# Causal mask of the diagonal score blocks added by VectorE instead of by TensorE, with another plan of the stretches and a norm's scale on GpSimd

## The chip, the cores and the metric

One core of one Trainium2 chip runs the whole program in one launch. The metric is the device time of one execution in microseconds (us), and lower is better. TensorE (PE), VectorE (DVE), ScalarE (ACT), GpSimd (POOL) and SyncE (SP, which here only issues transfers) each run their own instruction stream in order and wait for each other by semaphores.

## What is computed

```python
xn = _layernorm(x)                              # x: (4, 1024, 1024) float32
# attention: 32 query heads, 8 key/value heads, head size 32, causal
q, k, v = rope(xn @ wq.T), rope(xn @ wk.T), xn @ wv.T      # split into heads
scores = einsum('bhtd,bhsd->bhts', q, k) / sqrt(32)
scores = scores + triu(full((T, T), -inf), k=1)
s = (einsum('bhts,bhsd->bhtd', softmax(scores), v)) @ wo.T
# gate: a small recurrence on the last position of each batch row
x_norm = layer_norm(xn, in_gamma, in_beta)
thought = x_norm[:, -1, :] @ agg_w + agg_b      # (4, 1024)
for _ in range(4):
    t = layer_norm(thought, pn_gamma, pn_beta)
    t = gelu(t @ d1_w + d1_b)                   # 1024 -> 4096
    thought = thought + (t @ d2_w + d2_b)       # 4096 -> 1024
broadcast = (thought @ bc_w + bc_b)[:, None, :]
g = silu(layer_norm(xn + sigmoid(xn @ gate_w + gate_b) * broadcast, out_gamma, out_beta))
return x + s * g
```

## The kernel before

There are three phases: `project_phase` (norm, transposes and the projections to q, k, v, left in DRAM), `attention_phase` (attention, with the recurrence on `thought` woven into it), and `output_phase` (gate, output projection, norm, result). The change lies in the second.

The attention phase has 32 **turns**, one for each pair of a batch row and a key/value head, with its four query heads side by side. Turns come in pairs of one loop body (`par` 0 and 1); four pairs make one step of the recurrence, and four steps the phase. In a turn TensorE writes 36 **score blocks** into PSUM: block `u` is keys of tile `j` against queries of tile `i` (`i >= j`), 128 keys by 4 heads x 128 queries, 128x512 float32. They alternate between two banks `stp0` and `stp1` (`scores`, L1012). ScalarE takes the exponential of each block into `pr` (L800), and TensorE may write block `u + 2` only when the exponential of block `u` has released the bank. Eight of the 36 blocks are **diagonal** (`i == j`: blocks 0, 4, 7, 9, 26, 30, 33 and 35). For these TensorE adds the mask with a second product into the same bank, the identity times `mask_k` (L1015).

Everything else of a turn hangs in the gaps between score blocks. `PLAN_TEXT` says behind which block, its **slot**, each piece is issued, on TensorE and, in the same order of slots, on VectorE and ScalarE:

- `mx k`: the row maximum piece `k` (22 a turn, from 128x128 to 128x1024) is a product into `mxp0` or `mxp1` by TensorE (L999 to L1005) and a masked maximum by VectorE (L884). Piece `k` may be written when VectorE has released piece `k - 2`. Pieces 0 to 19 belong to the next turn, 20 and 21 to this one. `mt`: the maxima are transposed by TensorE, copied by ScalarE (L775) and moved by a DMA of SP (`qs<-mt`, L616) to where the next score blocks read them as an extra row.
- `pv half j`: probabilities times values (L1024). `cy`: ScalarE copies their sum out.
- `ss half`: TensorE sums the probabilities over the keys (L1033), and `rc half`: VectorE inverts them (L869 to L874). GpSimd adds the probability pieces up before that (L727, L741, L751: seven additions of half 1 and three of half 0) and multiplies the output by the inverse (L720).
- `fa`, `fb`, `fc`, `fs`, `ft`: one chunk of the recurrence's matrix products (L1055), its partial sums (L891) and its transpose; VectorE then adds the bias (`hpre`, L965) or adds to `th` (L967). `ge`: ScalarE's Gelu, with a table load on either side, in turns of `par` 0.
- `ls`, `l0`, `lc`, `l1`, `lv`, `lt`: the norm at a step's end, in the last turn of each step. `lt` is its last part: with `rs` (the reciprocal deviation, GpSimd, L715) VectorE scales, multiplies by gamma and adds beta (L861 to L863), and TensorE's first `fa` of the next turn needs the result `t_in`.

The program on VectorE is one stream: an instruction that waits holds all behind it.

Of the kernel before, what the change touches and what calls it, by code (L numbers as in the profile page):

```python
# [10 lines left out]
ALU = mybir.AluOpType  # L11
# [56 lines left out]
PLAN_TEXT = """  # L68
0: mx 20
1: pv 1 6, pv 1 7, cy 1  # L70
2: mx 21
3: fa 0, fa 1, fc
5: mx 0
6: mt 1, pv 0 0
7: mx 1
8: mx 2
9: fb 0, fb 1, fs
11: mx 3, pv 0 1, pv 0 2
12: mx 4
13: ft, pv 0 3, cy 0  # L80
14: mx 5, ls
15: mx 6
16: ss 1, rc 1
17: mx 7
18: pv 1 0
19: mx 8, l0, lc, ge
20: mx 9
21: ss 0, rc 0
22: mx 10
23: mx 11, pv 1 1, pv 1 2  # L90
24: mx 12, l1, lv
25: mx 13
26: mt 0
27: mx 14
28: mx 15, pv 1 3
29: mx 16
30: mx 17
31: pv 1 4
32: mx 18, lt
34: mx 19, pv 1 5  # L100
"""
# [27 lines left out]
def build_kernel(nc, x, wqT, wkT, wvT, woT, in_g, in_b, agg_w, agg_b, pn_g, pn_b, d1_w, d1_b, d2_w, d2_b,  # L129
                 bc_b, gate_w, gate_b, out_g, out_b, rope_c, rope_s, pick, out):  # L130
    def dram(name, shape, dt):
        return nc.dram_tensor(name, shape, dt, kind="Internal").ap()

    xt_d = dram("xt_scratch", (B, 2, P, KT, T), F32)

    q_d = dram("q_scratch", (B * PAIRS, 2, 2, P, T), F32)
    k_d = dram("k_scratch", (B, 2, 2, P, T), F32)
    v_d = dram("v_scratch", (GROUPS, P, NT, HD), F32)
    y_d = dram("y_scratch", (1 + GROUPS, P, T), F32)

    with ExitStack() as outer:
        def osb(name, shape, dt):
            return outer.enter_context(nc.sbuf_tensor(name, shape, dt))

        ident = osb("ident", [P, P], F32)
        ident16 = osb("ident16", [P, P], BF16)
# [4 lines left out]
        project_phase(nc, x, wqT, wkT, wvT, rope_c, rope_s, xt_d, q_d, k_d, v_d,  # L151
                      ident, ident16, mask_q, mask_k, mhalf)
        bcast = osb("bcast", [P, B, D], F32)
        attention_phase(nc, x, in_g, in_b, agg_w, agg_b, pn_g, pn_b, d1_w, d1_b, d2_w, d2_b, bc_b, pick,
                        q_d, k_d, v_d, y_d, ident, ident16, mask_q, mask_k, mhalf, bcast)
        output_phase(nc, x, woT, gate_w, gate_b, out_g, out_b, xt_d, y_d, mhalf, bcast, out)


def project_phase(nc, x, wqT, wkT, wvT, rope_c, rope_s, xt_d, q_d, k_d, v_d,
                  ident, ident16, mask_q, mask_k, mhalf):  # L160

# [5 lines left out]
    with ExitStack() as ctx:  # L167
# [95 lines left out]
        def _(pool):  # L263
# [10 lines left out]
                                    pattern=[[1, P]], channel_multiplier=-1).then_inc(const_ready, 1)  # L274
            pool.wait_ge(const_ready, 7)
            nc.gpsimd.tensor_copy(ident16[:], ident[:]).then_inc(const_ready, 1)

# [134 lines left out]
        def _(pe):  # L412
# [18 lines left out]
            ws = (w1, w2)  # L431
            pe.wait_ge(const_ready, 8)
            for k in range(KT):
# [40 lines left out]
def attention_phase(nc, x, in_g, in_b, agg_w, agg_b, pn_g, pn_b, d1_w, d1_b, d2_w, d2_b, bc_b, pick,  # L474
                    q_d, k_d, v_d, y_d, ident, ident16, mask_q, mask_k, mhalf, bcast):

# [6 lines left out]
    with ExitStack() as ctx:  # L483
# [211 lines left out]
        def _(pool):  # L695
# [34 lines left out]
            def turn(s, c, par, use):  # L730
# [12 lines left out]
                for j in (1, 2, 3, 4):  # L743
# [10 lines left out]
                    if j == 2:  # L754
                        normalise(0, n)
                    if j == 3 and "l1" in use:
                        ln_pool(s + 1, tb + use["l1"])

# [7 lines left out]
        def _(act):  # L766
# [18 lines left out]
            def turn(s, c, par, use):  # L785
# [3 lines left out]
                for u, (half, j, i) in enumerate(ST):  # L789
                    act.wait_ge(st_done, NST * n + u + 2)  # L790
                    if u == 0:
# [36 lines left out]
        def _(dve):  # L828
# [30 lines left out]
            def layernorm_scale(k, base):  # L859
                dve.wait_ge(ln_rs, k + 1)  # L860
                link(nc.vector.tensor_tensor(cen[:], cen[:], rows(rs[:]), ALU.mult), base)  # L861
                link(nc.vector.tensor_tensor(cen[:], cen[:], bc(fvec[:, 1, :], B), ALU.mult), base)
                nc.vector.tensor_tensor(t_in[:, :, 0:B], cen[:], bc(fvec[:, 2, :], B), ALU.add).then_inc(t_done, 1)  # L863

# [58 lines left out]
            for k in range(MX_LATE + 1):  # L923
# [6 lines left out]
                elif step == 1:  # L930
                    add_burst(3)
                elif step == 2:
                    chunk_out(4, 0)
                    dve.wait_ge(c_in, 16 * 12)
                    link(nc.vector.tensor_tensor(th[:], fr[:], bc(fvec[:, 0, :], B), ALU.add), 0)
                    layernorm_sum()
                elif step == 3:
                    layernorm_centre(5, 0)
                elif step == 4:
                    layernorm_var(6)  # L940
                    layernorm_scale(0, 0)
                if k < MX_LATE:
                    row_max(k, k, 0)
            BASE = links["n"]
            def turn(s, c, par, use):
# [6 lines left out]
                for slot in PLAN:  # L952
                    for e in slot:
                        if e[0] == "mx":
                            ahead = e[1] < MX_LATE
                            row_max(e[1], (n + ahead) * NMX + e[1], 1 - par if ahead else par)
                        elif e[0] == "rc":
                            reciprocals(e[1], n, tb + use[("ss", e[1])])
# [29 lines left out]
        def _(pe):  # L988
# [467 lines left out]
```

## Time and profile before

| | |
|---|---|
| median of 3 runs | 2692.56 us (2688.55 to 2693.68) |
| profiled execution, its time | 2689.99 us |
| its span, first to last instruction | 2687.9 us |
| busy in the span | PE 2545.3, DVE 1761.2, POOL 1370.4, ACT 994.7 us |
| attention phase, about | 606 to 1924 us, with a tail to 1950 us |

A row of the time-ordered view gives the start, the duration, the engine, the line and operation, what is written and read, and in brackets how long the engine had been idle before it and which engine and line ended that. "Busy" of PE holds modelled ends of pipelined products, so that the distance from one start to the next tells more of a product's cost than its duration does.

### The profile page before, as it was taken

To read this page: it belongs to the slowest core of one execution; us is meant where nothing else is said; L and a number is where in the kernel's file an instruction comes from. 1 tells how busy PE (TensorE), PEld (TensorE's weight loads), DVE (VectorE), ACT (ScalarE), POOL (GpSimd) and SP (SyncE) were. 2 spreads that over 40 slices of the span, in tenths; PEclk is the share of its full clock that TensorE was granted. 3 is DMA by queue.
4 is the path that set the end of the run, shared out by engine and by line. 5 is a ranking of instruction groups with operands and counts; after the bars stand their busy time and mean duration, and the time that the engine had idled before them with its cause. 6 is when DMAs were issued, how large, how long until landed. Compare 5 with 4: busy or idle time off the path is not lost. (4 is left out here: it accounts for less than half of the span.)

```text
span 2687.9 us, 45256 instructions
## 1 busy us (share of the span) xinstructions
PE 2545.3 (95%) x14205; PEld 1684.8 (63%) x14205; DVE 1761.2 (66%) x3577; ACT 994.7 (37%) x1650; POOL 1370.4 (51%) x627
## 2 busy tenths in 40 slices
PE   5999999987999989999999999999859999999998
PEld 4888888873444444444444444444348888888886
DVE  6444444537676677677677677677657777777777
ACT  2111111112566656565566555666431111111111
POOL 1111111123888888988888897898711111111111
PEclk9999999997999999999999999999879999999999
DMA  6444444438456546555456645555375666656556
GB/s 245 170 180 179 167 162 163 161 124 259 147 169 198 170 143 200 164 163 187 146 168 194 185 146 181 169 160 185 115 234 119 125 123 117 117 117 117 117 117 124
DMA packets 229848, 432.05 MB, mean 161 GB/s; under 512 B 17252, under 2 KB 100340, under 8 KB 229736
## 3 DMA queue, kind: packets, MB, share of 16 engines
q1 hardware_dynamic: 156344, 378.75, 42.9%
q0 software_dynamic: 73392, 51.91, 12.9%
q8 instruction: 58, 0.95, 0.1%
q14 instruction: 54, 0.44, 0.1%
HBM read 316.56 MB, written 113.51 MB: 160 GB/s over the span
## 5 line engine op out<-in xcount | busy, mean ns | idle before, releaser
L884 DVE CUSTOM_DVE_ANT_0 bcast<-mxp,mask_q 128x128 f32<-128x128 f32 (+7 forms) x1054 | 751.7, 751 | 347.2 <-PE mxp L1005 179.8
L800 ACT ACTIVATE pr<-stp 128x512 f32<-128x512 f32 x1152 | 665.0, 598 | 544.7 <-PE stp L1012 345.2
L1012 PE MATMUL stp<-qs,ks 97*128 97x512 f32 x1152 | 517.3, 460 | 27.8 <-ACT pr L800 19.5
L427 PE MATMUL eo<-xt,w 128*128 128x512 f32 x1920 | 448.5, 392 | 3.6 <-DVE xt L370 3.6
L751 POOL TENSOR_TENSOR acc<-acc,pr 128x2048 f32<-128x2048 f32 x96 | 440.1, 4585 | 7.5 <-POOL acc L751 4.4
L1012 PEld LDWEIGHTS stp<-qs,ks 97*128 97x128 f32 x1152 | 214.9, 189 | 356.3 <-ACT pr L800 253.8
L427 PEld LDWEIGHTS eo<-xt,w 128*128 128x128 f32 x1920 | 358.6, 189 | 77.3 <-issue 4.0
L1374 PE MATMUL gp<-g,xa 128*128 128x512 f32 x1536 | 355.8, 391 | 17.3 <-DMA xa<-xt_scratch 17.3
L1374 PE MATMUL op<-o,ya 128*128 128x512 f32 x1536 | 355.9, 391 | 10.2 <-DVE ya L1317 10.2
L1374 PEld LDWEIGHTS gp<-g,xa 128*128 128x128 f32 x1536 | 290.0, 189 | 78.4 <-DMA xa<-xt_scratch 18.1
L1374 PEld LDWEIGHTS op<-o,ya 128*128 128x128 f32 x1536 | 290.1, 189 | 70.9 <-DVE ya L1317 10.6
L1024 PE MATMUL yp<-pr,vs 128*32 128x512 f32 (+3 forms) x3088 | 315.6, 505 | 0.9 <-ACT pr L800 0.7
L727 POOL TENSOR_TENSOR acc<-acc,pr 128x1536 f32<-128x1536 f32 (+2 forms) x99 | 235.5, 2379 | 16.8 <-PE yp L1103 9.0
L292 POOL TENSOR_TENSOR r<-rt,r 128x1024 fp32r<-128x1024 f32 x40 | 96.0, 2399 | 282.0 <-ACT r L323 282.0
L1268 POOL DMA_DIRECT2D yr<-y_scratch x33 | 30.5, 924 | 363.8 <-issue 313.6
L751 POOL TENSOR_TENSOR acc<-pr 128x2048 f32<-128x2048 f32 x32 | 146.5, 4579 | 114.7 <-ACT pr L800 114.7
L396 DVE TENSOR_TENSOR rt<-eo,cs 128x512 f32<-128x512 f32 x160 | 99.0, 680 | 146.6 <-PE eo L427 146.6
L1002 PE MATMUL mxp<-ks,qs 96*128 96x512 f32 x394 | 178.2, 452 | 5.8 <-DVE mx L884 5.5
L323 ACT ACTIVATE r<-rt 128x1024 fp32r<-128x1024 f32 x40 | 42.4, 1060 | 355.4 <-DVE rt L400 350.8
L1301 ACT ACTIVATE c<-a 128x1024 f32<-128x1024 f32 x32 | 33.9, 1061 | 344.4 <-DVE a L1353 344.4
L1005 PE MATMUL mxp<-ks,qs 96*128 96x256 f32 (+2 forms) x528 | 127.9, 345 | 20.7 <-DMA qs<-q_scratch 16.2
L1024 PEld LDWEIGHTS yp<-pr,vs 128*32 128x32 f32 x3088 | 71.9, 110 | 114.6 <-issue 62.8
(143 smaller groups left out, 2991.0 us busy)
## 6 DMA issues: line engine op xcount, KB each, us to landing
wch<-in_d_w SPq DMA_DIRECT2D x132, 1024.0 KB, 10.0
qs<-q_scratch SPq DMA_DIRECT2D x201, 256.0 KB, 7.3
xa<-xt_scratch POOLq DMA_DIRECT2D x66, 512.0 KB, 6.3
xt_scratch<-xt SPq DMA_DIRECT2D x16, 2048.0 KB, 14.0
q_scratch<-r SPq DMA_DIRECT2D x64, 512.0 KB, 3.2
yr<-y_scratch POOLq DMA_DIRECT2D x33, 512.0 KB, 5.9
xs<-in_x SPq DMA_DIRECT2D x33, 512.0 KB, 5.5
y_scratch<-ys SPq DMA_DIRECT2D x65, 256.0 KB, 2.1
```

The lines of the kernel that those rows point to most:

```text
L292: nc.gpsimd.tensor_tensor(r2[:], rt[:, 0:2, :], f32(r1[:]), ALU.subtract).then_inc(r2_done, 1)
L396: last = nc.vector.tensor_tensor(rt[:, o, :], bank[:, e, :], cs[:, s, tok], ALU.mult)
L427: last = nc.tensor.matmul(out, lhs[a](k), rhs[c](k), start=(k == 0 and (a, c) == (0, 0)), stop=(k == KT - 1 and (a, c) == (1, 0)))
L727: nc.gpsimd.tensor_tensor(acc[:, :, c0:HALF], acc[:, :, c0:HALF], pr[1][:, :, at:at + HALF - c0], ALU.add).then_inc(add_done, 1)
L751: nc.gpsimd.tensor_tensor(acc[:], other, pr[1][:, :, at:at + HALF], ALU.add).then_inc(add_done, 1)
L800: nc.scalar.activation(pr[half][:, :, at:at + P], stp[u % 2][:].rearrange("p (h t) -> p h t", h=REP), ACT.Exp, scale=SCALE).then_inc(act_d ...
L884: last = nc.vector.tensor_tensor_reduce(out=bcast[:, k % 2, hh * step:hh * step + w], in0=mxp[k % 2][:, hh * step + c0:hh * step + c0 + w] ...
L1002: nc.tensor.matmul(bank[:, 0:512], lhs, ks[par][0:QR, 0:512], start=True, stop=True)
L1005: last = nc.tensor.matmul(bank[:, hh * step:hh * step + w], lhs, ks[par][0:QR, 0:w], start=True, stop=True)
L1012: last = nc.tensor.matmul(bank, ks[par][:, j * P:(j + 1) * P], qs[par][:, i // 4, :, (i % 4) * P:(i % 4 + 1) * P], start=True, stop=i != j)
L1024: last = nc.tensor.matmul(yp[h * HD:(h + 1) * HD, c0:HALF], vs[par][:, j, :], pr[half][:, h, at:at + HALF - c0], start=(j == 0), stop=(j = ...
L1374: last = nc.tensor.matmul(bank[:, cols], lhs[pa][:, k, :], ws[pw][:, k, cols], start=(k == 0 and (pa, pw) == (0, 0)), stop=(k == KT - 1 an ...
```

## The change

The mask product is gone from `scores`. Each diagonal block gets a plan entry `dm u` at its own slot: VectorE waits for the block, adds `mask_k` to it in PSUM in place (128x512, both banks as the block falls), and ScalarE's exponential waits for this instead of for TensorE. The bfloat16 identity `ident16` and its copy at the start go. The three instructions of `lt` go from VectorE to GpSimd, right behind L715, and the whole group now stands one addition earlier there (behind the second large addition instead of the third). The plan is written anew: most pieces stand at other slots.

```diff
@@ plan (two lines of each) @@
-9: fb 0, fb 1, fs
-13: ft, pv 0 3, cy 0
+9: dm 9, mx 3, mx 4
+10: ft, pv 0 0
...
@@ GpSimd @@
             def ln_pool(k, tu):
                 pool.wait_ge(tr_free, tu + 2)
                 nc.gpsimd.tensor_tensor(rs[:], ve[:], mhalf[:], ALU.pow).then_inc(ln_rs, 1)
+                pool.wait_ge(ln_rs, 3 * k + 1)
+                nc.gpsimd.tensor_tensor(cen[:], cen[:], rs[:].unsqueeze(1).to_broadcast([P, KT, B]),
+                                        ALU.mult).then_inc(ln_rs, 1)
+                pool.wait_ge(ln_rs, 3 * k + 2)
+                nc.gpsimd.tensor_tensor(cen[:], cen[:], fvec[:, 1, :].unsqueeze(2).to_broadcast([P, KT, B]),
+                                        ALU.mult).then_inc(ln_rs, 1)
+                pool.wait_ge(ln_rs, 3 * k + 3)
+                nc.gpsimd.tensor_tensor(t_in[:, :, 0:B], cen[:], fvec[:, 2, :].unsqueeze(2).to_broadcast([P, KT, B]),
+                                        ALU.add).then_inc(t_done, 1)
...
                     if j == 2:
                         normalise(0, n)
-                    if j == 3 and "l1" in use:
-                        ln_pool(s + 1, tb + use["l1"])
+                        if "l1" in use:
+                            ln_pool(s + 1, tb + use["l1"])
...
@@ ScalarE @@
-                    act.wait_ge(st_done, NST * n + u + 2)
+                    if i == j:
+                        act.wait_ge(dm_done, len(DIAG) * n + DIAG.index(u) + 1)
+                    else:
+                        act.wait_ge(st_done, NST * n + u + 2)
...
@@ VectorE @@
+                        elif e[0] == "dm":
+                            bank = stp[e[1] % 2][:].rearrange("p (h t) -> p h t", h=REP)
+                            dve.wait_ge(st_done, NST * n + e[1] + 2)
+                            nc.vector.tensor_tensor(bank, bank, mask_k[:].unsqueeze(1).to_broadcast([P, REP, P]),
+                                                    ALU.add).then_inc(dm_done, 1)
...
@@ TensorE @@
-                last = nc.tensor.matmul(bank, ks[par][:, j * P:(j + 1) * P], qs[par][:, i // 4, :, (i % 4) * P:(i % 4 + 1) * P],
-                                        start=True, stop=i != j)
-                if i == j:
-                    last = nc.tensor.matmul(bank, ident16[:], mask_k[:].unsqueeze(1).to_broadcast([P, REP, P]),
-                                            start=False, stop=True)
-                last.then_inc(st_done, 1)
+                nc.tensor.matmul(bank, ks[par][:, j * P:(j + 1) * P], qs[par][:, i // 4, :, (i % 4) * P:(i % 4 + 1) * P],
+                                 start=True, stop=True).then_inc(st_done, 1)
```

TensorE's stream of a `par` 0 turn of the kernel before, blocks 8 and 9 and what stands behind them. L1012 is a score block, L1015 the mask product, L1055 the chunk's products (`fb`).

```order
L1005 MATMUL mxp<-ks,qs 128x384 x2
L1010 REGISTER_ALU
L1012 MATMUL stp<-qs,ks 128x512
L1015 MATMUL stp<-mask_k,ident 128x512
L1038 REGISTER_ALU
L1055 MATMUL trp<-wch,t_in 32x512 x8
L1010 REGISTER_ALU
L1012 MATMUL stp<-qs,ks 128x512
```

The same engine and the same block 9 in the changed kernel, where a score block is L1019 and a row maximum product L1012. L1067 is the transpose `ft` and L1027 is `pv 0 0`.

```order
L1019 MATMUL stp<-qs,ks 128x512
L1000 REGISTER_ALU
L1012 MATMUL mxp<-ks,qs 128x384 x2
L1000 REGISTER_ALU
L1012 MATMUL mxp<-ks,qs 128x512 x2
L1017 REGISTER_ALU
L1019 MATMUL stp<-qs,ks 128x512
L1041 REGISTER_ALU
L1067 MATMUL trp<-ident,fsb 128x128 x4
L1127 ISA
L1027 MATMUL yp<-pr,vs 32x512 x4
```

Behind block 9 the chunk's products are gone (half of them stands at slot 6 and half at slot 7), the mask product is gone, and two row maxima and the transpose stand there.

VectorE's stream of the changed kernel around the same place: L964 is the new mask addition of block 9, L889 a row maximum, L903 reads the transpose and L974 is `hpre` (L965 before). Before, `hpre` stood at slot 13, behind three row maxima more than `fs`.

```order
L896 TENSOR_TENSOR fsb<-trp,fsb 128x512
L963 REGISTER_ALU
L964 TENSOR_TENSOR stp<-stp,mask_k 128x512
L884 REGISTER_ALU
L889 ISA bcast,mx<-mxp,mask_q 128x384
L889 ISA mx 128x1
...
L903 TENSOR_REDUCE fr<-trp 128x16 x2
L905 REGISTER_ALU
L973 ISA
L974 TENSOR_TENSOR hpre<-fr,b1c 128x32
```

The addition stands right in front of `mx 3` and `mx 4`, and `hpre` right behind these two.

GpSimd's stream of the changed kernel at a step's end, behind the second large addition (L759) and the product with the inverse (L728):

```order
L759 TENSOR_TENSOR acc<-acc,pr 128x2048
L726 REGISTER_ALU
L728 TENSOR_TENSOR ys<-ys,rinv 128x512
L713 REGISTER_ALU
L714 TENSOR_TENSOR f_rs<-f_ve,mhalf 128x4
L715 ISA
L716 TENSOR_TENSOR cen<-cen,f_rs 128x32
L718 REGISTER_ALU
L719 TENSOR_TENSOR cen<-cen,fvec 128x32
L721 REGISTER_ALU
L722 TENSOR_TENSOR t_in<-cen,fvec 128x8x4
```

Before, only the first of the four (`f_rs`) stood on this engine, one large addition later, and the other three on VectorE between two row maxima of slots 31 and 34.

## Rows read from the trace of the kernel before

**Rows 1.** The page: busy time, share of the span, instructions.

```profile
PE 2545.3 (95%) x14205; PEld 1684.8 (63%) x14205; DVE 1761.2 (66%) x3577; ACT 994.7 (37%) x1650; POOL 1370.4 (51%) x627
```

**Rows 2.** Busy time by stretch: span, PE, PEld, DVE, ACT, POOL, granted clock, DMA share.

```profile
768.00:846.00 78.00, 76.29 (x502) 37.55 (x501) 54.86 (x150) 46.88 (x85) 70.23 (x25) 1.00 0.57 176
...
924.00:1012.00 88.00, 81.01 (x507) 38.90 (x505) 63.49 (x157) 47.80 (x87) 72.71 (x26) 0.96 0.52 158
```

**Rows 3.** SP in order of time: one load of vs per turn, as a turn marker.

```profile
769.21 0.35 SPq L585 DMA_DIRECT2D vs<-v_scratch  x1
...
847.01 0.35 SPq L585 DMA_DIRECT2D vs<-v_scratch  x1
...
924.64 0.46 SPq L585 DMA_DIRECT2D vs<-v_scratch  x1
...
1012.38 0.35 SPq L585 DMA_DIRECT2D vs<-v_scratch  x1
```

**Rows 4.** TensorE in order of time: the waits of a pair of turns.

```profile
826.15 0.44 PE L999 MATMUL mxp<-ks,qs 96*128 96x384 f32 x1 [0.43 <-DVE mx L884]
...
829.86 0.50 PE L1012 MATMUL stp<-qs,ks 97*128 97x512 f32 x1 [1.12 <-ACT pr L800]
```

**Rows 5.** ScalarE in order of time: the first of two loads before that wait.

```profile
826.37 1.28 ACT L818 ACT_TABLE_LOAD   x1
```

**Rows 6.** Groups by form, 606 to 1924 us: count, busy us, mean ns, idle.

```profile
L751 POOL TENSOR_TENSOR acc<-acc,pr 128x2048 f32<-128x2048 f32 x96 | 440.1, 4585 | 7.5 <-POOL acc L751 4.4 <-ACT pr L800 1.1
...
L1015 PE MATMUL stp<-mask_k,ident 128*128 128x512 bf16 x256 | 101.2, 395 | 0.0
...
L884 DVE CUSTOM_DVE_ANT_0 bcast<-mxp,mask_q 128x512 f32<-128x512 f32 x132 | 85.8, 687 | 39.2 <-PE mxp L1005 38.6
...
L891 DVE TENSOR_TENSOR fsb<-trp,fsb 128x512 f32<-128x512 f32 x33 | 22.8, 692 | 12.9 <-PE trp L1055 12.9
```

**Rows 7.** TensorE and ScalarE in order of time: blocks 26 and 28, a `pv`.

```profile
1037.21 0.41 PE L1012 MATMUL stp<-qs,ks 97*128 97x512 f32 x1
1037.47 0.39 PE L1015 MATMUL stp<-mask_k,ident 128*128 128x512 bf16 x1
...
1038.54 0.51 PE L1012 MATMUL stp<-qs,ks 97*128 97x512 f32 x1
...
1039.48 1.06 PE L1024 MATMUL yp<-pr,vs 128*32 128x512 f32 x8
...
1037.89 0.60 ACT L800 ACTIVATE pr<-stp 128x512 f32<-128x512 f32 x1 [0.23 <-PE stp L1015]
```

**Rows 8.** GpSimd in order of time: late additions, and its wait in each turn.

```profile
1009.08 7.32 POOL L727 TENSOR_TENSOR acc<-acc,pr 128x1536 f32<-128x1536 f32 x3
...
1029.06 4.59 POOL L751 TENSOR_TENSOR acc<-pr 128x2048 f32<-128x2048 f32 x1 [4.84 <-ACT pr L800]
```

**Rows 9.** VectorE in order of time: `th` and `hpre` in two normal turns.

```profile
782.78 0.19 DVE L967 TENSOR_TENSOR th<-th,fr 128x32 f32<-128x32 f32 x1
...
820.94 0.72 DVE L965 TENSOR_TENSOR hpre<-fr,b1c 128x32 f32<-128x32 f32 x1
```

**Rows 10.** A step's end in order of time: GpSimd, VectorE, TensorE.

```profile
958.57 4.53 POOL L751 TENSOR_TENSOR acc<-acc,pr 128x2048 f32<-128x2048 f32 x1
...
944.71 1.39 DVE L852 TENSOR_TENSOR sq<-cen 128x32 f32<-128x32 f32 x1
...
959.65 3.50 DVE L861 TENSOR_TENSOR cen<-cen,f_rs 128x32 f32<-128x32 f32 x1
...
963.58 0.58 PE L1012 MATMUL stp<-qs,ks 97*128 97x512 f32 x1 [2.65 <-issue]
```

**Rows 11.** The tail in order of time: TensorE, and GpSimd's last product.

```profile
1922.88 0.39 PE L1015 MATMUL stp<-mask_k,ident 128*128 128x512 bf16 x1
...
1931.59 3.64 PE L1055 MATMUL trp<-wch,h_in 128*32 128x512 f32 x16 [6.77 <-DVE h_in L981]
...
1943.59 1.27 POOL L720 TENSOR_TENSOR ys<-ys,rinv 128x512 f32<-128x512 f32 x1 [10.67 <-DVE rinv L874]
```

More of the change, by code:

```diff
@@ L51 @@
 HALF_ST = len(score_units(0))
+DIAG = [u for u, (_, j, i) in enumerate(ST) if i == j]
 LAST_UNIT = {(half, j): u for u, (half, j, _) in enumerate(ST)}
@@ L68 @@
 PLAN_TEXT = """
[L69 to L76, printed above, removed]
-9: fb 0, fb 1, fs
-11: mx 3, pv 0 1, pv 0 2
-12: mx 4
-13: ft, pv 0 3, cy 0
[L81 to L86, printed above, removed]
-20: mx 9
[L88 to L100, printed above, removed]
+0: dm 0, mx 20, fa 0, fa 1
+1: mx 21, fc
+2: pv 1 6
+4: pv 1 7, mt 1, dm 4, mx 0
+5: cy 1, mx 1
+6: fb 0
+7: dm 7, mx 2, fb 1
+8: fs
+9: dm 9, mx 3, mx 4
+10: ft, pv 0 0
+12: mx 5, ls
+13: mx 6
+14: ss 1
+16: pv 0 1
+17: rc 1
+18: mx 7, mx 8, l0, lc
+19: pv 0 2
+20: mx 9
+21: mx 10
+22: pv 0 3
+23: cy 0
+24: mx 11, mx 12
+26: ss 0, dm 26, rc 0, pv 1 0
+27: mx 13, l1, lv
+28: ge, mx 14
+29: pv 1 1, pv 1 2
+30: dm 30, mx 15, mx 16
+31: pv 1 3
+32: mx 17, mt 0
+33: dm 33, mx 18
+34: pv 1 4, pv 1 5
+35: dm 35, mx 19
 """
@@ L145, in build_kernel @@
         ident = osb("ident", [P, P], F32)
-        ident16 = osb("ident16", [P, P], BF16)
         mask_q = osb("mask_q", [P, T], BF16)
@@ L151, in build_kernel @@
         project_phase(nc, x, wqT, wkT, wvT, rope_c, rope_s, xt_d, q_d, k_d, v_d,
-                      ident, ident16, mask_q, mask_k, mhalf)
+                      ident, mask_q, mask_k, mhalf)
         bcast = osb("bcast", [P, B, D], F32)
         attention_phase(nc, x, in_g, in_b, agg_w, agg_b, pn_g, pn_b, d1_w, d1_b, d2_w, d2_b, bc_b, pick,
-                        q_d, k_d, v_d, y_d, ident, ident16, mask_q, mask_k, mhalf, bcast)
+                        q_d, k_d, v_d, y_d, ident, mask_q, mask_k, mhalf, bcast)
         output_phase(nc, x, woT, gate_w, gate_b, out_g, out_b, xt_d, y_d, mhalf, bcast, out)
 def project_phase(nc, x, wqT, wkT, wvT, rope_c, rope_s, xt_d, q_d, k_d, v_d,
-                  ident, ident16, mask_q, mask_k, mhalf):
+                  ident, mask_q, mask_k, mhalf):
     NB = 2 * B
@@ L274, in _ @@
                                     pattern=[[1, P]], channel_multiplier=-1).then_inc(const_ready, 1)
-            pool.wait_ge(const_ready, 7)
-            nc.gpsimd.tensor_copy(ident16[:], ident[:]).then_inc(const_ready, 1)
             def rstd_of(n):
@@ L431, in _ @@
             ws = (w1, w2)
-            pe.wait_ge(const_ready, 8)
+            pe.wait_ge(const_ready, 7)
             for k in range(KT):
@@ L474, in attention_phase @@
 def attention_phase(nc, x, in_g, in_b, agg_w, agg_b, pn_g, pn_b, d1_w, d1_b, d2_w, d2_b, bc_b, pick,
-                    q_d, k_d, v_d, y_d, ident, ident16, mask_q, mask_k, mhalf, bcast):
+                    q_d, k_d, v_d, y_d, ident, mask_q, mask_k, mhalf, bcast):
     QR = 3 * HD
@@ L548, in attention_phase @@
         st_done, act_done, add_done, add0_done = sem("a_st"), sem("a_act"), sem("a_add"), sem("a_add0")
+        dm_done = sem("a_dm")
         mx_done, mx_free = sem("a_mx"), sem("a_mx_free")
@@ L857, in layernorm_var @@
                 nc.vector.tensor_scalar(ve[:], trp[:, 0:B], EPS_F, None, ALU.add).then_inc(tr_free, 1)
[L859 to L863, printed above, removed]
             def reciprocals(half, k, tu):
@@ L940, in _ @@
                     layernorm_var(6)
-                    layernorm_scale(0, 0)
                 if k < MX_LATE:
@@ L974, in turn @@
                             layernorm_var(tb + use["l1"])
-                        elif e[0] == "lt" and "l1" in use:
-                            layernorm_scale(s + 1, base)
                 if par == 1:
@@ L1183 @@
 LINKS_TURN = 1
-LINKS_STEP = 4
+LINKS_STEP = 2
 def output_phase(nc, x, woT, gate_w, gate_b, out_g, out_b, xt_d, y_d, mhalf, bcast, out):
```

## Prediction, made before the changed kernel ran

> **What bounds the kernel now.** I read the page first, then the busy time by stretch, then one engine after the other in order of time. The page [rows 1] has PE busy for 95% of the span, DVE for 66%, POOL for 51%. The stretches [rows 2] put that right: POOL hardly works outside the attention phase. In an undisturbed stretch of 78 us, which is a pair of turns, PE is busy 76.3 us, POOL 70.2, DVE 54.9, ACT 46.9. The change touches the bound, TensorE, but GpSimd stands close behind. The turn markers [rows 3] give 77.80 us for a normal pair (769.21 to 847.01), 38.9 a turn, and 87.74 for the pair that holds a step's end (924.64 to 1012.38), 9.9 more, at a mean clock of 0.96 instead of 1.00 [rows 2]. There are three such ends inside the phase and a fourth in its tail.
>
> What PE waits for in a normal pair is little [rows 4]: 0.43 us for a row maximum and 1.12 us for ScalarE. The second follows Gelu [rows 5]: a table load of 1.28 us on either side of it stands in front of an exponential whose bank TensorE wants. The rest, 77.80 - 1.55 = 76.25 or 38.1 us a turn, is TensorE's own work.
>
> **The mask products.** Eight a turn, 256 in all [rows 6]. The mean of 395 ns is a duration with a pipeline in it. A block of the same 512 columns lets the next product start after 0.26 us (1037.21 to 1037.47 [rows 7]), so I take 0.24 for a mask product, between 0.21 (a tenth of the distance off for the change of weights) and 0.26. That is 1.9 us a turn. TensorE's own work falls to 38.1 - 1.9 = 36.2 us a turn.
>
> **The mask additions.** No row adds from PSUM into PSUM. The nearest reads PSUM and SBUF at the same size, 692 ns (L891 [rows 6]), and the row maximum of 512 columns with the same bfloat16 mask takes 687. I take 0.69. Below, nothing in the rows suggests less than 0.6; above, the bound is twice the row, 1.4. DVE's work goes from 54.86 / 2 = 27.4 to 27.4 + 8 x 0.69 = 32.9 us a turn. It still has 3 us to spare, but it is one stream, and TensorE and ScalarE now wait for it eight times more.
>
> The chain of a diagonal block grows. Before [rows 7]: block at 1037.21, mask at 1037.47, exponential 1037.89 to 1038.49, the block after next at 1038.54, so 1.33 us. After: about 0.45 until the block has ended, 0.69 for the addition, 0.60 for the exponential and some 0.10 of signals, 1.85 us, if VectorE is free. TensorE has to have 1.85 us of work from one block to the one after the next, or more where a row maximum (0.7 to 1.2) is ahead of the addition. I went through the new plan slot by slot. The prices: 0.24 for a block, 0.44 for a row maximum of middle size [rows 4], 1.06 for a `pv` or `ss` of full width [rows 7]. Up to the block after next, block 26 has 2 x 0.24 + 1.06 (`ss 0`) + 1.06 (`pv 1 0`) + 0.44 = 3.0 us; block 30 has 2 x 0.24 + 2 x 0.44 + 1.06 = 2.4; block 33 has 2 x 0.24 + 0.44 + 1.06 and the somewhat narrower `pv 1 5`, 2.7; block 0 has `fa`, which is longer than a `pv`. Block 9 has 2 x 0.24 + 2 x 0.44 + 1.06 and the transpose, 2.7; there VectorE comes late, since `mx 2`, `fs` and the addition stand in a row, and it just suffices. Blocks 4 and 7 have about 2 us, block 35 has the row maximum and `fa`. So a few tenths a turn remain exposed, not eight times 0.5. `mt` and its DMA through SP's queue come earlier for half 1 and later for half 0 (slot 32); some 3 us of TensorE work stand between that copy and the next turn, enough for the move. The loads of k, q and v are issued by the same conditions as before.
>
> **Gelu.** `ge` now stands behind block 28, where slots 29 to 31 have three `pv` and two `mx` besides three blocks, 3 x 1.06 + 2 x 0.44 + 3 x 0.24 = 4.8 us, against 2 x 1.28 us of loads, Gelu and one exponential. The 1.12 us per pair should go, and is in the figure above already, because I took the recorded waits off.
>
> **GpSimd's floor.** POOL has 70.23 / 2 = 35.1 us a turn, and some tenths between its instructions (7.5 us in front of 96 additions alone [rows 6]), so 35.4 to 36.0. What it waits now is up to 4.84 us a turn, for the exponential that opens half 1 [rows 8]. At TensorE's 36.2 that wait is gone nearly, and GpSimd works without a pause: the turn can't fall below about 36.
>
> **What that triggers.** VectorE's `hpre` took 0.72 us where `th`, of the same size, took 0.19 [rows 9]; `cen` took 3.50 and ended when GpSimd's addition of 958.57 + 4.53 = 963.10 did [rows 10]. Both read two tensors in SBUF. With GpSimd busy all the time, `hpre` and the addition to `th`, now at slot 10, fall on one of its additions of 1.3 to 3.5 us each turn, and `mx 5` and all behind it wait. The slack of slots 11 to 17 takes most of that; I count 0 to 1.5 us a turn, and 0.5 together with the exposed tenths. The sum for a normal turn is 36.2 + 0.5 = **36.7 us**, 2.2 less than 38.9, and 32 x 2.2 = 70 us.
>
> The Trainium skill (SBUF — State Buffer, "Who interferes with whom") says that a VectorE instruction with two SBUF inputs waits for a whole GpSimd instruction that reads SBUF, and one with at most one SBUF input never does. By that rule the trace's 3.50 is a lock, and the new mask addition (one input in PSUM) stays at its price; were it locked as `cen` is, eight waits of 1 to 4 us a turn would turn the sum into a loss of several hundred us.
>
> **The norm at a step's end.** Before, `cen` and the next of the three took about 3.5 us each behind GpSimd's additions, PE waited 2.65 us [rows 10] and more behind it, and the mean clock of the pair was 0.96 [rows 2]. On GpSimd they wait for no one. Their cost there is not in the trace; the additions go at 4585 ns for 2048 elements [rows 6], 2.2 ns each, so 32 elements are below 0.3 us and each with its hand-over below 1: one to three us a step, on an engine that has a little room in hand. But `sq` (1.39 us [rows 10]) reads two SBUF inputs and now stands at slot 18, just as GpSimd begins its 4.6 us addition: up to 3 us of VectorE held, and `ls` at slot 12 can be held too. Of the 9.9 us I take back 5, three times: 15 us, with 0 and 9.9 each as bounds.
>
> **The tail.** PE waited 6.77 us for `h_in`, queued on VectorE behind the same three instructions [rows 11]. That goes, but the last step then waits for GpSimd's late additions (7.32 us [rows 8]) to reach the last sums: GpSimd has less lead than before. From the last block (1922.88) to the last product by the inverse (1943.59) 20.7 us; I take 3 off.
>
> **Sum.** 2690 - 70 - 15 - 3 = 2602 us against the profiled execution of 2689.99. The median of the runs shown lies 2.6 us above that, so **2604 us**, 3.3% faster. The identity's copy at the start is worth nothing measurable.
>
> **Rivals.**
> - *At the floor* (15%): no lock hits and no tenths are exposed, 36.2 a turn, and the ends give all 9.9. 2690 - 86 - 30 - 4 = 2570, plus 2.6: 2573. For it: the slack of slots 11 to 17. Against: VectorE at 33 of 36 us in one stream.
> - *VectorE's queue* (24%): the lock on `hpre` and `th` lasts 2 to 3 us in most turns, or the additions come late behind row maxima, so that 37.7 or more is a turn, and the ends give nothing: 2690 - 38 - 3 + 2.6 = 2652. For it: rows 9 and 10. Against: a turn made longer lets GpSimd get ahead, so that the next `hpre` meets a shorter addition.
> - *No change* (3%): the exposed waits eat exactly the 2.8 us a turn.
> - *Slower* (8%): the exposed chain at the diagonal blocks. If each of the eight costs the 0.5 us by which it is longer and half a row maximum (0.5) in front of the addition, a turn gains 8 and loses 2.7: 38.9 + 5.3, and 2690 + 32 x 5.3 = 2860. It decides from 2.7 / 8 = 0.34 us per block on. Against: the work that stands behind each diagonal block in the plan.
> - My forecast, 36.3 to 37.4 a turn, 2590 to 2626: 50%.
>
> **Numbers.** A measurement of this kernel can tell about 0.2%, 5 us. The range reaches to the floor and to VectorE's queue: 2570 to 2652, with a tenth or so outside on each side. Faster 0.89, same 0.03, slower 0.08.
>
> **What the profile after would show.** No L1015 row; PE near 36.2 us a turn of work. If I am right: turn markers at 36.3 to 37.4 us, without the 1.12 us wait behind Gelu; POOL busy above 34.5 of 36.7 us and its wait for the exponential under 1 us; mask additions at 0.69 us; no TensorE wait over 1 us in a normal turn; `hpre` often above 0.72; a step's end less than 6 us longer than a normal pair; `sq` at 2 us or more. Wrong would be: mask additions of 1 us and more, or TensorE idle in front of the block after each diagonal one (the exposed chain), or a wait for `mx` at slots 18 to 24 of a us or more in each turn (the lock).

## The result and the profile after

The changed kernel takes 2674.16 us (median of 7 runs, 2667.57 to 2679.28) against 2692.56 before (7 runs, 2688.55 to 2697.55): a ratio of 0.9929 (0.9914 to 0.9945), 0.7% faster. The forecast was 2604, and its range ended at 2652.

The page, with the lines that answer to [rows 1] and [rows 6], and the queue that brings instructions (packets, MB, share):

```profile
PE 2516.4 (94%) x13949; PEld 1667.3 (62%) x13949; DVE 1918.4 (72%) x3818; ACT 997.6 (37%) x1650; POOL 1373.6 (51%) x641
...
q14 instruction: 95, 0.78, 0.1%
...
L811 ACT ACTIVATE pr<-stp 128x512 f32<-128x512 f32 x1152 | 659.5, 597 | 513.9 <-DVE stp L964 326.9
...
L964 DVE TENSOR_TENSOR stp<-stp,mask_k 128x512 f32<-128x512 f32 x256 | 178.3, 696 | 80.3 <-PE stp L1019 44.0
```

The 256 mask products are gone and PE is busy for 28.9 us less in all, at a price of 0.696 us of VectorE for each addition, as forecast. The instruction queue moved 95 packets; its row in the page of before has 54:

```profile
q14 instruction: 54, 0.44, 0.1%
```

Next, SyncE's turn markers, which answer to [rows 3]:

```profile
764.73 0.35 SPq L584 DMA_DIRECT2D vs<-v_scratch  x1
...
806.72 0.36 SPq L584 DMA_DIRECT2D vs<-v_scratch  x1
845.25 0.35 SPq L584 DMA_DIRECT2D vs<-v_scratch  x1
882.51 0.35 SPq L584 DMA_DIRECT2D vs<-v_scratch  x1
920.08 0.35 SPq L584 DMA_DIRECT2D vs<-v_scratch  x1
966.85 0.36 SPq L584 DMA_DIRECT2D vs<-v_scratch  x1
1003.86 0.35 SPq L584 DMA_DIRECT2D vs<-v_scratch  x1
```

Turns are no longer alike. From 845.25 on they take 37.26 and 37.57 us, 74.83 the pair against 77.80 before. The pair ahead of them takes 41.99 and 38.53, 80.52. The pair with the step's end takes 83.78, 8.95 more than a good one. Busy time by stretch, with the columns of [rows 2]:

```profile
845.25:920.08 74.83, 73.23 (x486) 36.02 (x486) 66.84 (x165) 47.22 (x85) 70.70 (x25) 1.00 0.60 184
764.73:845.25 80.52, 75.93 (x486) 36.99 (x485) 66.16 (x165) 47.13 (x85) 70.01 (x25) 0.96 0.55 171
797.00:817.00 20.00, 16.82 (x94) 7.88 (x93) 12.68 (x42) 8.68 (x17) 15.46 (x7) 0.83 0.66 196
920.08:1003.86 83.78, 78.11 (x490) 37.46 (x490) 68.30 (x171) 47.22 (x85) 70.98 (x29) 0.94 0.55 165
```

The long pair does the same 486 products in 2.7 us more of busy time at clock 0.96, and is idle for 3 us more. In the 20 us around 807 the mean granted clock is 0.83, which is about 7 us at the lower level (1.2 GHz) and the rest at 2.4. What happened there, in order of time on three engines:

```profile
799.61 0.40 PE L1010 MATMUL mxp<-ks,qs 96*128 96x512 f32 x1
803.19 0.58 PE L1019 MATMUL stp<-qs,ks 97*128 97x512 f32 x1 [3.18 <-ACT pr L811]
...
801.64 0.70 DVE L964 TENSOR_TENSOR stp<-stp,mask_k 128x512 f32<-128x512 f32 x1 [3.68 <-issue]
...
802.54 1.09 ACT L811 ACTIVATE pr<-stp 128x512 f32<-128x512 f32 x2 [5.11 <-DVE stp L964]
```

Read it backwards. TensorE stood 3.18 us for an exponential; ScalarE stood 5.11 us for a mask addition; VectorE stood 3.68 us for "issue", that is, for nothing that the trace holds. The addition is the first instruction of a pair of turns (`dm 0`), the place where VectorE's loop jumps back. The phase has eight such jumps inside its steps. At six of them VectorE stands 3.5 to 3.9 us in front of the addition and TensorE then waits 2.8 to 3.4 us; at the first jump of the first and of the third step it is 2.1 and 2.0 us, and 1.4 and 1.3 us of TensorE.

Other rows in order of time, for the steps of the prediction: a normal pair's waits of TensorE (as [rows 4]), `th` beside GpSimd's addition (as [rows 9]), a step's end (as [rows 10]) and the tail (as [rows 11]):

```profile
754.74 0.50 PE L1019 MATMUL stp<-qs,ks 97*128 97x512 f32 x1 [0.72 <-ACT pr L811]
780.16 0.44 PE L1006 MATMUL mxp<-ks,qs 96*128 96x384 f32 x1 [0.68 <-DVE mx L889]
...
772.89 2.38 POOL L749 TENSOR_TENSOR acc<-acc,pr 128x1024 f32<-128x1024 f32 x1 [0.16 <-POOL acc L749]
...
772.98 2.34 DVE L976 TENSOR_TENSOR th<-th,fr 128x32 f32<-128x32 f32 x1
...
936.18 1.73 DVE L863 TENSOR_TENSOR sq<-cen 128x32 f32<-128x32 f32 x1
...
948.00 0.24 POOL L716 TENSOR_TENSOR cen<-cen,f_rs 128x32 f32<-128x32 f32 x1
948.31 0.24 POOL L719 TENSOR_TENSOR cen<-cen,fvec 128x32 f32<-128x32 f32 x1
948.63 0.24 POOL L722 TENSOR_TENSOR t_in<-cen,fvec 128x32 f32<-128x32 f32 x1
...
958.70 0.79 PE L1019 MATMUL stp<-qs,ks 97*128 97x512 f32 x1 [3.57 <-issue]
...
1912.76 3.61 PE L1058 MATMUL trp<-wch,h_in 128*32 128x512 f32 x16 [0.97 <-DVE h_in L988]
...
1923.33 1.27 POOL L728 TENSOR_TENSOR ys<-ys,rinv 128x512 f32<-128x512 f32 x1 [3.16 <-DVE rinv L879]
```

`th` needs 0.19 us alone and here 2.34, ending with GpSimd's addition. The three instructions of the norm take 0.24 us each on GpSimd. TensorE's wait for `h_in` shrank from 6.77 to 0.97 us. At the step's end TensorE still waits for "issue", 3.57 us where it was 2.65.

### The profile page after: what moved, and what is told of

Its sections match the earlier page's. It is cut to its first block and busy times, and to the rows that moved or that the text cites. A ratio compares the mean times of both kernels' runs of the same rounds, so it can differ in the third digit from the quotient of the medians.

```text
span 2668.1 us, 45287 instructions
## 1 busy us (share of the span) xinstructions
PE 2516.4 (94%) x13949; PEld 1667.3 (62%) x13949; DVE 1918.4 (72%) x3818; ACT 997.6 (37%) x1650; POOL 1373.6 (51%) x641
## 5 line engine op out<-in xcount | busy, mean ns | idle before, releaser
L889 DVE CUSTOM_DVE_ANT_0 bcast<-mxp,mask_q 128x128 f32<-128x128 f32 (+7 forms) x1054 | 749.8, 750 | 110.6 <-PE mxp L1010 67.3
L1019 PE MATMUL stp<-qs,ks 97*128 97x512 f32 x1152 | 493.9, 459 | 43.9 <-ACT pr L811 33.6
L1019 PEld LDWEIGHTS stp<-qs,ks 97*128 97x128 f32 x1152 | 213.0, 191 | 397.1 <-ACT pr L811 210.6
L759 POOL TENSOR_TENSOR acc<-acc,pr 128x2048 f32<-128x2048 f32 x96 | 440.5, 4588 | 5.1 <-POOL acc L759 5.1
L1027 PE MATMUL yp<-pr,vs 128*32 128x512 f32 (+3 forms) x3088 | 318.5, 500 | 0.9 <-ACT pr L811 0.9
L964 DVE TENSOR_TENSOR stp<-stp,mask_k 128x512 f32<-128x512 f32 x256 | 178.3, 696 | 80.3 <-PE stp L1019 44.0
L1271 POOL DMA_DIRECT2D yr<-y_scratch x33 | 30.5, 924 | 365.0 <-issue 346.0
L759 POOL TENSOR_TENSOR acc<-pr 128x2048 f32<-128x2048 f32 x32 | 146.6, 4583 | 72.5 <-ACT pr L811 72.5
L1009 PE MATMUL mxp<-ks,qs 96*128 96x512 f32 x394 | 162.5, 416 | 5.8 <-DVE mx L889 5.5
L1027 PEld LDWEIGHTS yp<-pr,vs 128*32 128x32 f32 x3088 | 71.3, 109 | 140.3 <-issue 115.8
```

What stands on the lines that cost most here:

```text
L759: nc.gpsimd.tensor_tensor(acc[:], other, pr[1][:, :, at:at + HALF], ALU.add).then_inc(add_done, 1)
L889: last = nc.vector.tensor_tensor_reduce(out=bcast[:, k % 2, hh * step:hh * step + w], in0=mxp[k % 2][:, hh * step + c0:hh * step + c0 + w] ...
L964: nc.vector.tensor_tensor(bank, bank, mask_k[:].unsqueeze(1).to_broadcast([P, REP, P]), ALU.add).then_inc(dm_done, 1)
L1009: nc.tensor.matmul(bank[:, 0:512], lhs, ks[par][0:QR, 0:512], start=True, stop=True)
L1027: last = nc.tensor.matmul(yp[h * HD:(h + 1) * HD, c0:HALF], vs[par][:, j, :], pr[half][:, h, at:at + HALF - c0], start=(j == 0), stop=(j = ...
```

## The experiments

The theory after reading the two traces: VectorE's loop body grew from 258 to 290 instructions, so that at each jump back its first instructions are no longer in the store it issues from, and the rest is as forecast. The rival: VectorE is just too full, and `dm 0` is late because it stands behind row maxima. The numbers below count VectorE's instructions in the built program; the body stands at 437 to 695 before and at 434 to 724 after. Every kernel here computes the whole result.

### Moving the body without touching the work: e1_pad60 and e3_before_pad60

```diff
@@ VectorE, ahead of the loops: in the changed kernel (e1), in the kernel before (e3) @@
+            for _ in range(60):
+                nc.vector.engine_nop()
             dve.wait_ge(xl_in, 16)
```

> The changed kernel with 60 empty VectorE instructions ahead of the two loops (in a stretch where VectorE waits for a load), so that the loop body of 290 VectorE instructions lies elsewhere in the program. Theory F (fetch): at 8 jumps back of the inner loop VectorE stood still for 2.1 to 3.9 us because the jump's target was no longer in its instruction store, and the turns behind were 37.3 + up to 5 us; the excess of those turns over 37.3 sums to about 42 us. Moved, the jumps find their target: 2674 - 42 = 2632 us, no issue wait of VectorE but the three at a step's end. Theory W (a wait of data or signals at the turn's start that the view does not name: a late move of the maxima, the queue of mask additions): the empty instructions change nothing, 2674 us.

> The kernel before with the 60 empty instructions of the first run ahead of its loops, as a control. Theory F: the body of 258 does not miss where it stands and does not where it is moved to; within 4 us of 2692.6. Theory W: the same. A gain of 10 us or more would say that the fetch costs the kernel before something too.

Sixty instructions that do nothing made the changed kernel 51 us faster (47 us by the two ratios to the kernel before): 2623.49 us (2618.77 to 2626.79), 0.9756 (0.9739 to 0.9773). On the kernel before they did nothing: 2687.61, 0.9991 (0.9982 to 1.0001). Busy time from the first to the last turn marker, first of the changed kernel:

```profile
606.00:1874.88 1268.88, 1201.85 (x7658) 584.99 (x7659) 1065.15 (x2642) 735.97 (x1326) 1100.05 (x395) 0.96 0.57 177
```

and of e1, whose body stands at 494 to 784:

```profile
606.00:1826.00 1220.00, 1175.40 (x7658) 574.80 (x7659) 1058.66 (x2645) 735.52 (x1326) 1100.13 (x395) 0.98 0.60 184
```

The same 7658 products take 48.9 us less: 26.4 in busy time, with the mean clock at 0.98 instead of 0.96, and 22.5 in waits. The waits of TensorE by what they waited for (us in total, times, longest), in the changed kernel:

```profile
PE stp L1019 <- ACT pr L811: 33.6, 25, 3.4
PE stp L1019 <- issue: 10.3, 3, 3.6
```

and in e1:

```profile
PE stp L1021 <- ACT pr L811: 11.6, 16, 0.7
PE stp L1021 <- issue: 10.5, 3, 3.7
```

The waits for an exponential fell by 22.0 us and their longest from 3.4 to 0.7; VectorE has no more "issue" at the eight jumps; e1's instruction queue moved 52 packets. The eight pairs of turns behind the jumps now take 74.6 to 74.7 us where they took 76.5 to 82.2, 42 us less in all; the other 7 us between the first and the last marker lie in the remaining turns, 3 of them at the step ends. A turn without a step's end takes 37.1 us. The rival is refuted: the work and its order are the same. The three turns at the step ends stay long (45.36, 44.24 and 44.52 us).

### Where the border lies: e5_pad256 and e13_pad3

```diff
@@ e5; e13 the same with 3 @@
+            for _ in range(256):
+                nc.vector.engine_nop()
```

> The changed kernel with 256 empty VectorE instructions ahead of the loops instead of 60. Theory F, made sharper by the four runs so far: the store is filled in blocks of 256 instructions, and a loop misses when its body reaches over three of them. It did with the body at 434 to 724 and at 437 to 727, and did not at 494 to 784, 437 to 695 and 434 to 692. Moved by a whole block, to 690 to 980, it lies as the changed kernel's does: the issue waits of about 2 to 4 us at the 8 inner jumps are back, and the time is 2674 us within 6, plus what the empty instructions hold up at the start (0 to 5). Rival: any move away from the old place helps (a matter of warm-up or of the time between the first instructions): 2623 us as with 60.

> The changed kernel with 3 empty VectorE instructions ahead of the loops, as many as the norm's move took out there, so that the body starts at 437, where the kernel before has it. If the longer body (290 instead of 258) makes it reach a third block, the misses stay, as they were there with 437 to 727 in the kernel before: 2674 us within 6. If the three missing instructions had moved it over an edge: 2623 us.

Were it the length of the lead-in, 256 would help as 60 did. It didn't: 2683.99 us, 0.9976 (0.9965 to 0.9987), with the waits for "issue" back (3.2 to 3.9 us at all eight jumps) and 97 packets; 7.7 us of it are in the first turn (52.51 us against 44.85), which the empty instructions hold up. Three more, which put the body where it began before (437), gave 2676.80 us, 0.9945 (0.9925 to 0.9965), waits of 3.4 to 4.1 us and 95 packets. So it isn't the three instructions that left the lead-in either, but the 32 that came into the body. Bodies at 434 to 724, 437 to 727 and 690 to 980 wait; 437 to 695, 434 to 692 (e4) and 494 to 784 don't. Borders every 256 instructions, one of them between 440 and 468 of this count, fit all six: the bodies that wait reach over two borders, into three blocks.

The Trainium skill (Runtime: NRT & Kernel Launch, "Instruction fetch mechanics") describes a store of two blocks of 256 instructions for an engine such as VectorE, filled ahead in order, and a fetch when a jump's target is outside. The runs agree, with a lead-in of unknown length ahead of the first counted instruction; the block's size itself was not measured. At the jumps of these kernels VectorE stood 2.0 to 4.1 us.

### The long body on the kernel before: e2_before_body32

```diff
@@ VectorE, kernel before, 32 instructions a pair @@
+                        if e == ("mx", 0):
+                            for _ in range(16):
+                                nc.vector.engine_nop()
```

> The kernel before, with 16 empty VectorE instructions a turn in front of mx 0, where VectorE idles 2 us anyway: the inner loop's body grows from 258 to 290 VectorE instructions, as many as in the changed kernel, and nothing else changes. Theory F: VectorE stands still at the 8 jumps back of the inner loop, and the time rises by 8 x 3 to 5 us: 2692.6 + 24 to 40 = 2717 to 2733 us. Theory W: within 3 us of 2692.6.

This body stands at 437 to 727, as e13's does. The fetch came and the cost did not: 2684.75 us, 0.9988 (0.9979 to 0.9997). The instruction queue moved 95 packets, and VectorE stood 2.1 to 2.3 us at all eight jumps, one of them in order of time:

```profile
806.72 1.23 DVE L884 CUSTOM_DVE_ANT_0 bcast<-mxp,mask_q 128x1024 f32<-128x1024 f32 x1 [2.11 <-issue]
```

At the jump the old plan has only row maxima 20 and 21 on VectorE. In the trace of the kernel before, VectorE idles 1.15 us in front of the first, 0.70 in front of the second and 2.24 in front of the next one, all of them waits for TensorE's products, so that a standstill of 2.1 us fits into time that was idle anyway. The expectation of a loss was wrong: a standstill costs only what it is queued in front of. One reservation: these standstills are also shorter than the changed kernel's 3.5 to 3.9 us, and no run has the old plan with a standstill of that length.

### Taking the parts of the change away: e4_mask_on_pe and e12_mask_pe_body32

```diff
@@ e4: changed kernel, mask product back on TensorE (plan and norm stay as changed) @@
-4: pv 1 7, mt 1, dm 4, mx 0
+4: pv 1 7, mt 1, mx 0
...
+                if i == j:
+                    last = nc.tensor.matmul(bank, ident16[:], mask_k[:].unsqueeze(1).to_broadcast([P, REP, P]),
+                                            start=False, stop=True)
@@ e12: e4 with the 16 empty instructions of e2 ahead of mx 0 @@
```

> The changed kernel, its plan and its norm on GpSimd kept, with the mask product back on TensorE (the dm entries leave the plan, the body shrinks to 258 VectorE instructions). TensorE has 1.9 us a turn more. Theory F: no issue waits at the inner jumps, a turn of about 38.3 to 38.6 us, and 2660 to 2675 us, so that the whole gain of the changed kernel could be had without moving the mask. Theory W: the stalls at the turn's start, if they come from the plan, stay, and it is 2700 us or more; if they come from the mask additions, they go.

> The run with the mask product back on TensorE under the new plan, with 16 empty VectorE instructions a turn in front of mx 0, so that the body lies at 434 to 724 as the changed kernel's does. Theory F says that VectorE stands still at each inner jump back; theory E (exposure) that this costs time only where ScalarE's exponentials of blocks 35 and 0 hang on VectorE: here only row maxima do, so 2650 us within 5. Rival: the stall costs whatever hangs on it, 2670 us or more.

e4, with a body of 258, took 2650.22 us, 0.9860 (0.9843 to 0.9876), less than expected: the plan and the norm on GpSimd alone gain some 39 us, at 37.97 us a turn. With the mask additions (and no fetch) e1 takes 27 less. The changed kernel's 18 us is what the fetch leaves of these two; that is the same medians subtracted in another order, and no check of them.

e12 then made e4's body as long as the changed kernel's, without its additions. I had expected little, on the theory that the fetch costs only through exponentials that wait for an addition. It took 2693.92, 1.0011 (1.0001 to 1.0022), 44 us more than e4. VectorE and TensorE in order of time at a jump:

```profile
806.83 1.23 DVE L889 CUSTOM_DVE_ANT_0 bcast<-mxp,mask_q 128x1024 f32<-128x1024 f32 x1 [4.10 <-issue]
...
809.34 0.27 PE L1052 MATMUL trp<-ident,mx 128*16 128x128 f32 x1 [2.28 <-DVE mx L889]
```

TensorE's waits for these maxima in total, and the busy time by stretch behind the jump shown and behind a later one:

```profile
PE trp L1052 <- DVE mx L889: 16.8, 8, 2.3
```

```profile
808.00:828.00 20.00, 18.62 (x114) 9.99 (x114) 15.69 (x54) 12.00 (x23) 14.56 (x7) 1.00 0.82 258
1128.00:1148.00 20.00, 18.75 (x96) 9.66 (x97) 13.65 (x47) 9.47 (x18) 11.88 (x6) 0.83 0.75 254
```

Here TensorE waits for the maxima of `mt 1`, which the new plan has at slot 4 and the old one had at slot 6. That theory fell. The new plan by itself had used up the slack at the jump. The profiled executions of e12 and e4 lie 39.6 us apart: TensorE waits 16.8 us at the eight jumps (1.6 to 2.3 us each) and is busy for 20.9 us more, with a mean granted clock of 0.83 in the 20 us behind three of the eight jumps and 1.00 behind the one shown. So under the new plan the fetch costs about as much without the mask additions as with them.

### The lock and the step's end: e7_psum, e8_steps, e9_both

```diff
@@ e7: e1, and the partial sums stay in PSUM, so that hpre and th read one tensor in SBUF @@
-                    last = nc.vector.tensor_reduce(fr[:, 4 * nb:4 * nb + 4, :], v[:, nb, :, 0:B, :], AX.X, ALU.add)
+                    last = nc.vector.tensor_reduce(v[:, nb, :, B:2 * B, 0], v[:, nb, :, 0:B, :], AX.X, ALU.add)
...
-                                nc.vector.tensor_tensor(hpre[:], fr[:], bc(b1c[:], B), ALU.add).then_inc(hp_done, 1)
+                                nc.vector.tensor_tensor(four(hpre[:]), part, four(bc(b1c[:], B)), ALU.add).then_inc(tr_free, 1)
@@ e8: e1, and the loop over the four steps written out, on every engine @@
-            with engine.Fori(0, STEPS) as s:
+            for s in range(STEPS):
@@ e9: both @@
```

> The run with 60 empty instructions, and the sums of a chunk (fr) left in PSUM, so that hpre and the addition to th have one SBUF input instead of two. Theory L (lock): these two no longer wait for GpSimd's additions (1 to 2.3 us a turn), 0.19 us each, and what TensorE waits behind them, 0.72 us for an exponential and 0.5 to 0.7 for a row maximum in each pair, goes: 16 x 1.0 to 1.4, so 2601 to 2608 us. Rival: the turn is held by GpSimd's 36 us or by the additions' own chain, and the waits only move: 2620 to 2624 us.

> The run with 60 empty instructions, and the outer loop over the four steps written out four times (the inner loops stay), so that no jump back is longer than an inner loop's body. Theory F: the 3.4 us issue wait of TensorE and the 4 us one of VectorE at the three step's ends go, with the fall of the clock behind them. Those turns are 44.2 to 45.4 us now instead of 37.1; they become about 38: 3 x 7 = 21 us less, 2602 us. Rival: the norm's own chain makes them long: 2618 to 2624 us.

> Both of the last two edits together, on the run with 60 empty instructions. If both theories hold the gains add up, 2623 - 18 - 21 = 2584 us; if GpSimd's 36 us a turn bound it, 32 turns of 36.3 us give no less than 2595.

e7 took 2600.43 us, 0.9663 (0.9650 to 0.9676), 23 less than e1, at 36.1 us a turn with hardly a deviation outside the step ends. A pair of it, and its `th`:

```profile
700.00:772.30 72.30, 72.30 (x485) 35.95 (x484) 63.14 (x165) 46.98 (x86) 70.09 (x25) 1.00 0.61 190
```

```profile
769.40 0.19 DVE L982 TENSOR_TENSOR th<-trp,th 128x32 f32<-128x32 f32 x1
```

PE has no gap left at 36.15 us a turn, and POOL is busy for 35.05 of them. `th` is back at 0.19 us although GpSimd works on, and VectorE's busy time fell from 66.28 us in a pair of e1 (727.39 to 801.63) to 63.14: the lock on `hpre` and `th` cost VectorE 1.6 us a turn, and the turn 1.0.

e8 took 2604.46 us, 0.9683 (0.9669 to 0.9696), 19 less than e1. Without the outer jump TensorE's three waits for "issue" at a step's end (3.4 to 3.7 us in e1) are gone, and these turns take 40.46, 40.61 and 40.57 us instead of 44 to 45, 12.5 of the 19 us. The loop was written out on every engine, so the run doesn't say how much of this is TensorE's jump and how much VectorE's, which had waits for "issue" of 4.08 and 3.91 us at two of e1's three step ends. Its markers around one end:

```profile
910.29 0.35 SPq L584 DMA_DIRECT2D vs<-v_scratch  x1
950.75 0.35 SPq L584 DMA_DIRECT2D vs<-v_scratch  x1
```

e9, with both, took **2579.14 us** (2578.36 to 2582.11), 0.9586 (0.9573 to 0.9599), 4.1% below the kernel before and the fastest here. The two gains add up: 2623 - 23 - 19 = 2581.

### The two safeguards of the change: e10_oldplan and e11_norm_dve

```diff
@@ e10: e1 with the plan of before, each dm at its block's slot (two lines) @@
-0: dm 0, mx 20, fa 0, fa 1
-1: mx 21, fc
+0: dm 0, mx 20
+1: pv 1 6, pv 1 7, cy 1
@@ e11: e1 with the norm's scale back on VectorE @@
-32: mx 17, mt 0
+32: mx 17, lt, mt 0
```

> The run with 60 empty instructions, with the plan of the kernel before (the mask additions at the start of their own slots, lt dropped since the norm's scale stays on GpSimd). What the new plan is worth to the mask additions. In the old plan blocks 0 and 4 have one row maximum or nothing behind them and block 35 nothing, so there the chain of 1.85 us is exposed; Gelu's 1.12 us a pair is back. Theory P (the plan carries the gain): 39 to 40.5 us a turn, 2690 to 2740 us. Rival: the additions hide in any plan, and a turn is the old 38.9 less the 1.9 of the products: 37 to 37.5 us, 2625 to 2640.

> The run with 60 empty instructions, with the norm's scale back on VectorE (behind mx 17 at slot 32). What the move to GpSimd is worth. Theory L: two of the three instructions wait for GpSimd's additions again, 3.5 us each, in front of the mask additions of blocks 33 and 35, and TensorE waits for most of it: 4 step ends by 4 to 7 us, 2640 to 2650 us. Rival: the step's end is held by the jump back of the outer loop, which takes its 3.4 us in either case and hides the rest: 2623 to 2630.

e10 took 2853.21 us, 1.0599 (1.0583 to 1.0615), some 44 us a turn and far above the 2690 to 2740 expected. TensorE's waits for an exponential in it, in total and one in order of time:

```profile
PE stp L1024 <- ACT pr L814: 152.0, 216, 1.5
```

```profile
1137.75 0.50 PE L1024 MATMUL stp<-qs,ks 97*128 97x512 f32 x1 [1.45 <-ACT pr L814]
```

216 waits of 0.7 us, seven a turn, are 4.75 us a turn, where e1 has 0.36. They are 4.4 of the 7.3 us by which a turn is longer than e1's on average; 2.6 more are not waits but longer busy time of the same products, the clock in the stretch from 1230 to 1318 being 0.93. This is the exposed chain of the rival "slower", and the new plan is what takes it away. The rival's 5.3 us a turn and 2860 us came out, but in part by luck: it had eight waits of 1.0 us and no loss of clock.

e11 took 2654.00 us, 0.9870 (0.9855 to 0.9885), 30.5 more than e1. VectorE in order of time at a step's end:

```profile
1257.81 4.47 DVE L863 TENSOR_TENSOR cen<-cen,f_rs 128x32 f32<-128x32 f32 x1
1262.32 0.19 DVE L864 TENSOR_TENSOR cen<-cen,fvec 128x32 f32<-128x32 f32 x1
1262.54 3.29 DVE L865 TENSOR_TENSOR t_in<-cen,fvec 128x32 f32<-128x32 f32 x1
```

Two of the three are held by GpSimd's additions. The three step ends take 22 us more than e1's (52.34, 53.97, 49.91 against 45.36, 44.24, 44.52). The profiled execution of e11 is 24 us longer than e1's, so the step ends are nearly all of that; the other three executions of e11 are 6 to 10 us longer still, and no trace shows where. Moving the norm is worth more than the 15 + 3 forecast, once GpSimd hardly pauses.

## Why the prediction was right and wrong

- **TensorE's own work, 36.2 us a turn:** right. e7 runs at 36.1.
- **Mask additions at 0.69 us, not locked:** right, 0.696; and no TensorE wait over 1 us in a turn without a jump (0.68 and 0.72 above).
- **Waits and lock, 0.5 us a turn:** too small. e1's 37.1 less e7's 36.1 is 1.0 us, which over 32 turns is 16 us more than forecast. The held instructions and their place were named rightly.
- **The mask product, 0.24 us between 0.21 and 0.26:** a tenth off 0.26 is 0.23 and not 0.21. The sum takes 0.24 and does not depend on it.
- **Gelu's 1.12 us goes:** right. **GpSimd's wait falls under 1 us:** nearly, 1.20 and 1.36 in turns without a jump, and some 3.9 behind a jump.
- **The step's end, 5 of 9.9 us taken back:** 1.0 at the first (9.94 to 8.95), 1.9 in the mean of the three (9.8 to 7.9), so some 6 us of the 15; "less than 6 us longer than a normal pair" was wrong. The norm did become cheap (0.24 us an instruction where a bound of 0.3 was taken; `sq` took 1.73, not 2 or more), but TensorE's wait for "issue" had been read as a consequence of the norm. e8 shows it to be the outer loop's jump: it stays with the norm moved and goes with the loop.
- **The tail, 3 us:** 6.7; from the start of the last score block to the product by the inverse are 14.3 us (1909.02 to 1923.33), against 21.1 (1922.54 to 1943.59).
- **The sum:** the steps of the forecast without the jump are measured by e1, 2623, within the likeliest case (2590 to 2626) and 19 us above the forecast: about 16 for the lock and 9 for the step ends, less 4 that the tail gave more.
- **The step that failed** is "32 x 2.2": it took 32 equal turns, and VectorE's stream as the durations of its instructions ("27.4 + 8 x 0.69, still 3 us to spare"). It did not ask what 32 more instructions do to a loop body. They made VectorE fetch at each of the eight jumps, with the addition that opens the turn right behind. That took 47 to 51 us, 42 of them in the eight pairs behind the jumps, 5.3 a jump; 2.8 of these are TensorE's wait for the exponential, and nearly all the rest the longer busy time of the same products, at a lower granted clock. None of the rivals held this mechanism; the trace before had the same signature at TensorE's outer jump, "2.65 <-issue".

What stays open: why VectorE stands 2.1 to 2.3 us at the jumps of e2 and 3.4 to 4.1 at those of e12 and e13, and 2.0 us at two of the changed kernel's. With e7 two of the step ends grew to 47 us. Their products are busy for 42.1 us at a mean clock of 0.89, where e1's second step end has 39.7 us at 0.96, which is most of the difference; why the clock is lower there stays open too.

## What to carry to other kernels

Where a change adds instructions to a loop body, count them engine by engine, and look for "issue" in front of the first instruction after the jump and at the packets of the instruction queue. What a standstill there costs is decided by what is queued behind it, so put nothing urgent first in the body; and try some empty instructions ahead of the loop, which costs one run. A wait for "issue" is no one's lateness: explain it by the engine's own stream before charging it to a neighbour.

## What the hardware showed that I had not expected

- A jump back of VectorE's loop kept VectorE standing for 2.0 to 4.1 us when the body of 290 instructions began at 434, 437 or 690, and not at all at 494. TensorE stood 3.4 to 3.7 us at the outer jump in e1, and not with the loop written out.
- A TensorE wait of 3.18 us stood in a stretch of 20 us (797 to 817) with a mean granted clock of 0.83, and the products took 26.4 us more over the phase than with the waits gone. Waits of nearly the same length went either way in e12: behind one of 2.28 us (808 to 828) the clock stayed at 1.00, around one of 2.12 us (1128 to 1148) it was 0.83, with 0.50, the lower level (1.2 GHz), from 1130 to 1135.
- GpSimd did three 128x32 operations in 0.24 us each, beside 0.19 for VectorE when it isn't held; VectorE held by GpSimd took 2.34 and 4.47 us for the same size. With one of the two inputs left in PSUM (e7), `th` took 0.19 us beside a busy GpSimd.
